# Residual additions moved to the end of DVE's step, and the last one split between ACT and POOL

## The chip, the cores and the metric

The kernel runs on one core of a Trainium2 chip. What is told is the device time of one execution in microseconds; lower is better. The core's engines work side by side: PE (TensorE) multiplies matrices, DVE (VectorE) and ACT (ScalarE) read and write SBUF and PSUM, POOL (GpSimd) works on SBUF, and SP (SyncE) issues transfers. Each runs its own list of instructions in order and waits on semaphores for the others.

## What is computed

x is 8 sequences of 512 tokens with 128 channels, all in float32. Two residual blocks follow each other. The first is a state space mixer with 32 heads, the second a feed-forward block that mixes each token with the one before it:

```python
x = L0_attn_x
x = x + _layernorm(_L0_attn_ref(_layernorm(x, axis=-1), ...), axis=-1)
x = x + _layernorm(_L0_ffn_ref(_layernorm(x, axis=-1), ...), axis=-1)

# in _L0_ffn_ref:
x_prev = jnp.concatenate([jnp.zeros((B, 1, C), x.dtype), x[:, :-1, :]], axis=1)
xr = mu_r * x + (1.0 - mu_r) * x_prev
xk = mu_k * x + (1.0 - mu_k) * x_prev
r = jax.nn.sigmoid(jnp.einsum('btc,dc->btd', xr, W_r))
k = jnp.einsum('btc,dc->btd', xk, W_k)
k_act = jnp.square(jax.nn.relu(k))
out = r * jnp.einsum('btc,dc->btd', k_act, W_v)
```

The mixer projects the normalised x to z (256 columns), a gated x (512), B and C (192) and per-head scalars, rotates B and C by accumulated angles, forms scores in chunks of tokens with a state carried from chunk to chunk, gates with z and projects back with W_out. The two layer norms of a block's result (`_layernorm(...)` behind each block) are what the names below call the factor of the first residual and the last normalisation.

## The kernel before, in words

**Tiles.** The tokens are cut in chunks of 64; a tile holds 64 tokens of two sequences on 128 partitions and 128 channels. There are 8 chunks c of 4 tiles (NQ = 4), 32 tiles n = 4 c + q. Each engine unrolls one `step` for each n. x, o (the projected result) and so on lie in SBUF for all tiles: `x_all`, `o_all`.

**The mixer, a pipeline over tiles.** In step n, PE projects x of tile n+1 (`project_x`, L876), turns B and C of tile n+1 (`turn`, L940, which waits for the mask of tile n), projects z, B and C of tile n+2 (`project_bc`, L868), turns y of n-1 (L1062), does the chunk's products of tile n (`mix`, L963 to L975), the scores of n+1 (L954), and the output product of n-1 (L1071), then a part of the feed-forward block. ACT in step n: copy and square of o (tile n-2, L693, L695), the gate of x of tile n+1 (`x_gate`, silu in PSUM, L667), `turned` (L678), the upper part of x of tile n+3 (L582), then a part of the feed-forward block (`empty_ffn_bank`), y turned (L683), squares of B and C of n+2 (L656, L658, behind DVE's `biased`), the gate of z (L673), the square of y (L688), and last `ffn(n)`. POOL in step n: the lower part of x (L430), `ffn(n)`, then factors of tile n+2 behind ACT's squares (L455, L458, L466), the scaling of z (`decayed_z`, L473), and the decay of the state (L481).

**DVE's step n, in order:** `mask` of tile n (L1405), `gated_y` of n-1 (L1424), `state` (L1413), `ffn(n)`, `weighted_x` x1 of tile n+1 (L1398, waits for ACT's gate and for POOL's factors), `biased` of n+2 (L1381), `weighted_x` xg of n+1 (L1398), in q = 3 `mix` (two instructions, L1509), and `rotations` of n+2 (two, L1386 and L1391, both with two inputs in SBUF).

**The feed-forward block, behind by chunks.** In step n = (c, q), DVE's `ffn` does: q = 0 `moments(c-2)` (L1488, L1490); q = 1 `norm_biases(c-2)` (L1499) and, from c = 4, `last_residual(c-4)` (L1531, four tiles: o_all = ff * rstd + x_all); q = 2 `factor_terms(c-1)`, `gated_v(c-3)` (L1518) and `stats3(c-3)` (L1525); q = 3 `residual(c-1)` (L1471, four tiles: x_all = o_all * factor + x_all) and `stats2(c-1)` (L1477), for c-1 from 0 to 5. `moments(k)` takes both the statistics of the residual of chunk k and those of the feed-forward result of chunk k-2; POOL raises them to -1/2 (`rstd`, L500), DVE forms the bias -mean * rstd. ACT's `ffn`: q = 0 `k_square`, q = 1 `normed(c-2)` (L731, scale and bias, four tiles), q = 2 `outputs(c-4)` (L774, four tiles: adds the bias to o_all), and in `empty_ffn_bank` q = 0 `k_relu`, q = 1 `gate_r`, q = 3 `scaled_behind(c-2)` (L746, two instructions). DVE's `mix(c-2)` in q = 3 waits for `scaled_behind`. PE in q = 3, after the step of the mixer, does `project_k` (L1114), which waits for `mix`; in q = 0 `project_r` (L1135).

**The end.** Chunk 7 is split in two units of two tiles, so there are 9 units; `residual(6)` stands behind step 30, and `last_ffn` on each engine holds what is left. `last_use(k)` and `rounds` say which earlier round used the columns of statistics that round k takes again, and so what `rstd`, `norm_biases` and `gated_v` wait for. SP stores a chunk when the count `outv` says that its four tiles are done.

## Time and profile before

| what | value |
|---|---|
| median of 3 runs | 247.10 us (246.79 to 247.14) |
| the profiled execution | 247.12 us |
| its span | 245.3 us |
| granted clock of PE, mean | 0.96 |
| busy: PE, DVE, ACT, POOL | 208.8, 210.7, 181.3, 142.4 us |

The page's second part shows the span in 40 slices, each digit the busy share in tenths:

```profile
PE   0895997589999999979979997999799799949930
PEld 0893443357777776758857875787588577627920
DVE  1799999987879987996999999999999998864880
ACT  2466685639988689778977896899789879747661
POOL 7444225646777696766757765766777576046230
```

The first 50 us load the inputs and build tables. From there to 211 us the 32 tiles run through the pipeline, with the granted clock at full. From about 120 us (chunk 3) every chunk has the same pattern. The last 34 us are the remainder of the feed-forward block. The chain that ended last, as the profile gives it, is only the last output operation, so the order of the waits has to be read from the timelines.

### The profile page before, as it was taken

The numbers are of one execution on the slowest core, as the hardware profiler recorded it, in microseconds if no ns is written. First come the engines' busy times: TensorE is split into PE (matmuls) and PEld (weight loads), VectorE is DVE, ScalarE is ACT, GpSimd is POOL, SyncE is SP. The second block draws the span as 40 slices with busy tenths as digits, with TensorE's granted clock in tenths as the row PEclk, the third lists the DMA queues.
The fourth block names the chain that finished last, engine by engine and source line by source line (L and its number), as shares of the span: only waits on it lengthen the run. The fifth ranks groups of instructions, "written<-read, shape, count | busy, mean of one in ns | idle before, by whom it ended". The sixth has DMA issues, their size and how long they took to land. (4 is left out here: it accounts for less than half of the span.)

```text
span 245.3 us, 6409 instructions
## 1 busy us (share of the span) xinstructions
PE 208.8 (85%) x1902; PEld 156.1 (64%) x1902; DVE 210.7 (86%) x658; ACT 181.3 (74%) x697; POOL 142.4 (58%) x241
## 2 busy tenths in 40 slices
PE   0895997589999999979979997999799799949930
PEld 0893443357777776758857875787588577627920
DVE  1799999987879987996999999999999998864880
ACT  2466685639988689778977896899789879747661
POOL 7444225646777696766757765766777576046230
PEclk9999799989999999999999999999999999986995
DMA  5980000000000000000000001001000100100223
GB/s 119 233 283 1 3 0 0 1 0 4 3 1 4 0 3 0 4 1 3 3 3 0 3 4 44 3 0 45 3 3 0 43 5 4 43 0 0 45 52 88
DMA packets 10199, 6.45 MB, mean 26 GB/s; under 512 B 864, under 2 KB 9856, under 8 KB 10160
## 3 DMA queue, kind: packets, MB, share of 16 engines
q1 hardware_dynamic: 10016, 5.77, 9.1%
q8 instruction: 18, 0.29, 0.5%
q0 software_dynamic: 144, 0.21, 0.4%
q14 instruction: 21, 0.17, 0.2%
HBM read 3.88 MB, written 2.10 MB: 24 GB/s over the span
## 5 line engine op out<-in xcount | busy, mean ns | idle before, releaser
L975 PE MATMUL bank<-x,sg 64*64 64x256 f32 x256 | 35.4, 396 | 0.0
L667 ACT ACTIVATE bank<-bank,rsn 128x512 f32<-128x512 f32 x32 | 21.1, 659 | 17.0 <-PE bank L876 17.0
L975 PE MATMUL bank<-xg,sg 64*64 64x256 f32 x256 | 33.0, 376 | 0.0
L963 PE MATMUL pair<-x,turned_bc 64*64 64x256 f32 x224 | 31.1, 397 | 0.0
L1398 DVE TENSOR_TENSOR x<-bank,wx 128x512 f32<-128x512 f32 x32 | 21.8, 682 | 7.3 <-ACT bank L667 7.3
L458 POOL TENSOR_TENSOR rb<-mse,halfn 128x2 f32<-128x2 f32 x32 | 24.8, 773 | 2.5
L500 POOL TENSOR_TENSOR frs<-fmo,halfn 128x8 f32<-128x8 f32 (+2 forms) x13 | 15.1, 1158 | 17.2 <-DVE fmo L1490 17.2
L1071 PE MATMUL bank<-wo_sb,yt 128*128 128x128 f32 x128 | 23.3, 306 | 1.9 <-ACT yt L683 1.9
L430 POOL TENSOR_TENSOR x_lo<-xnT_all,x_hi 128x128 fp32r<-128x128 f32 x32 | 14.8, 463 | 17.0 <-ACT x_hi L582 16.9
L656 ACT ACTIVATE junk<-bank 128x64 f32<-128x64 f32 x64 | 13.9, 228 | 11.2 <-DVE bc L1381 8.7
L975 PEld LDWEIGHTS bank<-xg,sg 64*64 64x64 f32 x256 | 18.0, 134 | 6.3 <-issue 0.2
L473 POOL TENSOR_TENSOR zs<-zs,ec_all 128x256 f32<-128x256 f32 x32 | 22.0, 687 | 0.0
L975 PEld LDWEIGHTS bank<-x,sg 64*64 64x64 f32 x256 | 15.4, 135 | 10.1 <-issue 6.1
L1398 DVE TENSOR_TENSOR xg<-bank,wx 128x512 f32<-128x512 f32 x32 | 21.7, 679 | 0.0
L455 POOL TENSOR_TENSOR mse<-msb,eps_all 128x2 f32<-128x2 f32 x32 | 7.4, 233 | 24.0 <-ACT junk L658 23.8
L481 POOL TENSOR_TENSOR st<-sp,f_all 128x256 f32<-128x256 f32 x28 | 18.1, 646 | 5.4 <-DVE sp L1413 5.4
L876 PE MATMUL bank<-w_hi,x_hi 128*128 128x512 f32 x32 | 17.2, 536 | 3.8 <-DVE w_lo L1282 2.7
L1071 PEld LDWEIGHTS bank<-wo_sb,yt 128*128 128x128 f32 x128 | 17.1, 194 | 4.7 <-ACT yt L683 2.1
L969 PE MATMUL bank<-st,bt 64*64 64x256 f32 x128 | 19.4, 379 | 0.6 <-DVE o_all L1333 0.6
L954 PEld LDWEIGHTS pair<-bt 64*64 64x64 f32 x256 | 16.9, 132 | 4.4
L954 PE MATMUL pair<-bt 64*64 64x64 f32 x256 | 18.0, 217 | 0.0
L1386 DVE TENSOR_TENSOR rot<-bc,cs_all 128x384 f32<-128x384 f32 x32 | 17.6, 550 | 0.0
(200 smaller groups left out, 712.0 us busy)
## 6 DMA issues: line engine op xcount, KB each, us to landing
x_all<-x SPq DMA_DIRECT2D x16, 128.0 KB, 3.7
out<-o_all SPq DMA_DIRECT2D x14, 128.0 KB, 2.5
cm<-consts SPq DMA_DIRECT2D x1, 640.0 KB, 5.6
w_sb<-w_in SPq DMA_DIRECT2D x1, 480.0 KB, 4.6
out<-o_all SPq DMA_DIRECT2D x4, 64.0 KB, 2.1
cm<-consts POOLq DMA_DIRECT2D x1, 128.0 KB, 3.9
wo_sb<-w_out SPq DMA_DIRECT2D x1, 128.0 KB, 4.7
bcb_sb<-bc_bias SPq DMA_DIRECT2D x1, 96.0 KB, 3.7
```

Of the source, the lines that this page charges most:

```text
L458: nc.gpsimd.tensor_tensor(rb[:, par], mse[:], halfn[:, 0:R], ALU.pow).then_inc(S["rb_ready"], 1)
L473: nc.gpsimd.tensor_tensor(zs[:, q].rearrange("p (h e) -> p h e", e=P), zs[:, q].rearrange("p (h e) -> p h e", e=P), at(ec_all, n).unsqueez ...
L481: nc.gpsimd.tensor_tensor(st[:, q].rearrange("p (h e) -> p h e", e=P), sp[:].rearrange("p (h e) -> p h e", e=P), at(f_all, i).unsqueeze(2) ...
L667: nc.scalar.activation(x_ps[:], x_ps[:], ACT.Silu, scale=rsn[:, par:par + 1]).then_inc(S["x_silu"], 1)
L876: mm = nc.tensor.matmul(x_ps[:], a[:, par], b[:, O_X:O_S], start=(k == 0), stop=(k == 2))
L954: mm = nc.tensor.matmul(scores[half(h), r], bt[half(r), par, r, half(h)], bt[half(r), par, 1 - r, half(h)], start=True, stop=True)
L963: mm = nc.tensor.matmul(p_ps[half(1 - h)], turned_bc[half(h), q, 2 * r], rx(x, r)[half(h)], start=(r == 0), stop=(r == R - 1))
L969: mm = nc.tensor.matmul(y_ps[par][half(h)], bt[half(1 - h), par, h, half(h)], state[half(1 - h)], start=True, stop=stop)
L975: mm = nc.tensor.matmul(y_ps[par][half(h)], sg[half(h), a, r], rx(x, r)[half(h)], start=start, stop=stop)
L1071: mm = nc.tensor.matmul(o_ps, yt[:, k], wo_sb[:, k], start=(k == 0), stop=(k == 1))
L1386: vec.tensor_tensor(rot[:], bc[:].rearrange("p (g a n) -> p g a n", g=G3, a=2).unsqueeze(3) .broadcast_to([128, G3, 2, 2, H]), at(cs_all, ...
L1398: vec.tensor_tensor((x1, xg)[a][:, par].rearrange("p (a e) -> p a e", e=P), x_ps[:].rearrange("p (a e) -> p a e", e=P), wx[:, par, a].unsq ...
```

## The change

- DVE's `residual(c-1)` leaves `ffn` in q = 3 and stands at the very end of DVE's step, behind `mix` and `rotations`.
- Its statistics, `stats2`, stand at the start of `ffn` in q = 0 of the next chunk, ahead of `moments`.
- For chunks 0, 1 and 2 (`POOL_UNITS = 3`) DVE's `last_residual` is not done. ACT, in place of `outputs`, writes the whole last normalisation `ff * rstd + bias` to o_all (`scaled_f`, four tiles), and POOL adds x_all to it (`add_residual`), two tiles in its `ffn` of q = 3 of the same chunk of steps and two in q = 1 of the next.
- The waits for `res`, the count of DVE's last residuals, are split by `wait_added`: for those chunks they are for ACT's new count `scaled_f`.
- All other work, and `last_ffn`, is as before.

```diff
--- before.py
+++ after.py
@@ -49,6 +49,7 @@
 
 FAC_STEPS = 3
 LAST_SPLIT = 2
+POOL_UNITS = 3
 MIX_UNITS = 6
 UNITS = [(c * NQ, c * NQ + NQ) for c in range(NC_ - 1)] + [(NT - NQ, NT - NQ + LAST_SPLIT), (NT - NQ + LAST_SPLIT, NT)]
 
@@ -293,7 +294,7 @@
         wv_half = sb("wv_half", 128, D)
         ff = sb("ff", 128, 2 * NQ, D)
         cnames = ("x1 stats agg mom pow norm_bias normed tr_ps tr_sb carried shifted scaled mixed last k_ps k_relu k_act r_ps th "
-                  "v_ps f stats3 res outv").split()
+                  "v_ps f stats3 scaled_f res outv").split()
         C = {n: sem("c_" + n) for n in cnames}
         s_mix = sem("mixing_weights")
         s_wo = sem("w_out_centred")
@@ -369,8 +370,15 @@
 
             for j in range(k - 1, -1, -1):
                 if rounds[j][0] < rounds[k][1] and rounds[k][0] < rounds[j][1]:
-                    return j + 1, hi(rounds[j][2]), hi(rounds[j][3])
-            return 0, 0, 0
+                    return j + 1, hi(rounds[j][2]), rounds[j][3]
+            return 0, 0, -1
+
+        def wait_added(eng, u):
+
+            if u < POOL_UNITS:
+                wait_past(eng, C["scaled_f"], hi(u))
+            else:
+                eng.wait_ge(C["res"], hi(u) - hi(POOL_UNITS - 1))
 
         def aggregated(k):
 
@@ -495,7 +503,7 @@
                 pool.wait_ge(C["mom"], k + 1)
                 wait_past(pool, C["norm_bias"], used)
                 wait_past(pool, C["normed"], n2)
-                wait_past(pool, C["res"], n3)
+                wait_added(pool, n3)
                 t = slice(rounds[k][0], rounds[k][1])
                 nc.gpsimd.tensor_tensor(frs[:, t], fmo[:, t], halfn[:, 0:t.stop - t.start], ALU.pow).then_inc(C["pow"], 1)
 
@@ -512,11 +520,17 @@
                 nc.gpsimd.tensor_tensor(prevT[:, B:, 0:1], curT[:, 0:B, L - 1:L],
                                         one[:].unsqueeze(1).broadcast_to([128, B, 1]), ALU.mult).then_inc(C["carried"], 1)
 
+            def add_residual(u, part):
+                for i in range(lo(u), hi(u))[part]:
+                    pool.wait_ge(C["scaled_f"], i + 1)
+                    pool.wait_ge(C["x1"], i + 1)
+                    nc.gpsimd.tensor_tensor(o_all[:, i], o_all[:, i], x_all[:, i], ALU.add).then_inc(C["outv"], 1)
+
             def pool_outputs(u, part):
                 pool.wait_ge(C["norm_bias"], round3(u) + 1)
                 pool.wait_ge(C["outv"], lo(u) + part.start)
                 for i in range(lo(u), hi(u))[part]:
-                    pool.wait_ge(C["res"], i + 1)
+                    pool.wait_ge(C["res"], i + 1 - hi(POOL_UNITS - 1))
                     nc.gpsimd.tensor_scalar(o_all[:, i], o_all[:, i], fnb[:, column3(i):column3(i) + 1], None,
                                             ALU.add).then_inc(C["outv"], 1)
 
@@ -528,6 +542,10 @@
                     carry_scaled(c - 2)
                 if q == 2 and valid(c - 1):
                     factors(c - 1)
+                if q == 3 and 0 <= c - 4 < POOL_UNITS:
+                    add_residual(c - 4, slice(0, 2))
+                if q == 1 and 0 <= c - 5 < POOL_UNITS:
+                    add_residual(c - 5, slice(2, 4))
 
             def last_ffn():
                 rstd(6)
@@ -766,11 +784,19 @@
                 act.wait_ge(C["k_relu"], u + 1)
                 nc.scalar.activation(ka[:, columns(u)], ka[:, columns(u)], ACT.Square).then_inc(C["k_act"], 1)
 
+            def scaled_f(u):
+                act.wait_ge(C["norm_bias"], round3(u) + 1)
+                act.wait_ge(C["x1"], hi(u))
+                for i in range(lo(u), hi(u)):
+                    k = column3(i)
+                    nc.scalar.activation(o_all[:, i], ff[:, slot(i)], ACT.Identity, scale=frs[:, k:k + 1],
+                                         bias=fnb[:, k:k + 1]).then_inc(C["scaled_f"], 1)
+
             def outputs(u):
                 act.wait_ge(C["norm_bias"], round3(u) + 1)
                 act.wait_ge(C["outv"], lo(u))
                 for i in range(lo(u), hi(u)):
-                    act.wait_ge(C["res"], i + 1)
+                    act.wait_ge(C["res"], i + 1 - hi(POOL_UNITS - 1))
                     nc.scalar.activation(o_all[:, i], o_all[:, i], ACT.Identity,
                                          bias=fnb[:, column3(i):column3(i) + 1]).then_inc(C["outv"], 1)
 
@@ -810,7 +836,7 @@
                 if q == 1 and valid(c - 2):
                     normed(c - 2)
                 if q == 2 and valid(c - 4):
-                    outputs(c - 4)
+                    (scaled_f if c - 4 < POOL_UNITS else outputs)(c - 4)
 
             act.wait_ge(S["st_zero"], 2)
             for n in range(-2, NT):
@@ -1494,7 +1520,9 @@
                 used, n2, n3 = last_use(k)
                 dve.wait_ge(C["pow"], k + 1)
                 wait_past(dve, C["normed"], n2)
-                wait_past(dve, C["outv"], n3)
+                wait_added(dve, n3)
+                if n3 >= POOL_UNITS:
+                    dve.wait_ge(C["outv"], hi(n3))
                 t = slice(rounds[k][0], rounds[k][1])
                 vec.scalar_tensor_tensor(out=fnb[:, t], in0=fag[:, t, 0], scalar=-1.0, in1=frs[:, t], op0=ALU.mult,
                                          op1=ALU.mult).then_inc(C["norm_bias"], 1)
@@ -1513,7 +1541,7 @@
             def gated_v(u):
                 dve.wait_ge(C["th"], u + 1)
                 dve.wait_ge(C["v_ps"], u + 1)
-                wait_past(dve, C["res"], hi(ahead(u)))
+                wait_added(dve, ahead(u))
                 for k, i in enumerate(range(lo(u), hi(u))):
                     vec.scalar_tensor_tensor(out=ff[:, slot(i)], in0=th[:, slot(i)], scalar=1.0,
                                              in1=ffn_bank("v", u)[:, k * D:k * D + D],
@@ -1534,19 +1562,18 @@
             def ffn(n):
                 c, q = divmod(n, NQ)
                 if q == 0 and valid(c - 2):
+                    if c - 2 < NC_ - 2:
+                        stats2(c - 2)
                     moments(c - 2)
                 if q == 1 and valid(c - 2):
                     norm_biases(c - 2)
-                if q == 1 and valid(c - 4):
+                if q == 1 and valid(c - 4) and c - 4 >= POOL_UNITS:
                     last_residual(c - 4)
                 if q == 2 and valid(c - 1):
                     factor_terms(c - 1)
                 if q == 2 and valid(c - 3):
                     gated_v(c - 3)
                     stats3(c - 3)
-                if q == 3 and 0 <= c - 1 < NC_ - 2:
-                    residual(c - 1)
-                    stats2(c - 1)
 
             def last_ffn(general):
                 stats2(6)
@@ -1609,6 +1636,8 @@
                     mix(n // NQ - 2)
                 if within(n + 2):
                     rotations(n + 2, (q + 2) % NQ)
+                if q == NQ - 1 and 0 <= n // NQ - 1 < NC_ - 2:
+                    residual(n // NQ - 1)
 
             biased(0)
```

## Rows read from the trace of the kernel before

**Rows 1.** The windows view: stretch, length, busy time of PE, PEld, DVE, ACT, POOL.

```profile
140.00:160.00 20.00, 18.72 (x199) 14.13 (x199) 19.86 (x60) 16.76 (x72) 13.98 (x24) 1.00 0.07 16
```

**Rows 2.** The waits view, 77 to 200 us: total idle, times, longest.

```profile
DVE x L1398 <- ACT bank L667: 4.1, 4, 1.8
...
PE bank L1114 <- DVE prevT L1509: 6.6, 5, 1.4
```

**Rows 3.** The timeline of DVE, chunk 3, q=1: start, duration, instruction, [idle before].

```profile
114.06 0.69 DVE L1398 TENSOR_TENSOR x<-bank,wx 128x512 f32<-128x512 f32 x1 [1.79 <-ACT bank L667]
```

**Rows 4.** The timeline of DVE, chunk 4 and the start of chunk 5.

```profile
134.45 2.03 DVE L1531 SCALAR_TENSOR_TENSOR o_all<-ff,frs,x_all 128x128 f32<-128x128 f32 x4
...
136.40 0.68 DVE L1398 TENSOR_TENSOR x<-bank,wx 128x512 f32<-128x512 f32 x1
...
138.72 0.42 DVE L1405 TENSOR_TENSOR sg<-pair,cm 128x256 f32<-128x256 f32 x1
...
141.96 0.67 DVE L1398 TENSOR_TENSOR x<-bank,wx 128x512 f32<-128x512 f32 x1
...
142.55 0.35 DVE L1381 TENSOR_TENSOR bc<-bank,bcb_sb 128x192 f32<-128x192 f32 x1
...
145.26 1.89 DVE L1471 SCALAR_TENSOR_TENSOR x_all<-o_all,tokc,x_all 128x128 f32<-128x128 f32 x4
...
147.07 0.86 DVE L1477 BATCH_NORM_STATS2 fst<-x_all 128x6 f32<-128x128 f32 x4
...
147.85 0.67 DVE L1398 TENSOR_TENSOR x<-bank,wx 128x512 f32<-128x512 f32 x1
...
149.30 0.74 DVE L1509 SCALAR_TENSOR_TENSOR curT<-bank,mu_sb,behind 128x512 f32<-128x512 f32 x1
...
151.56 0.41 DVE L1405 TENSOR_TENSOR sg<-pair,cm 128x256 f32<-128x256 f32 x1
...
152.56 0.63 DVE L1488 BATCH_NORM_AGGREGATE fag<-fst 128x2 f32<-128x6 f32 x8
...
153.38 0.69 DVE L1398 TENSOR_TENSOR x<-bank,wx 128x512 f32<-128x512 f32 x1
...
156.78 2.04 DVE L1531 SCALAR_TENSOR_TENSOR o_all<-ff,frs,x_all 128x128 f32<-128x128 f32 x4
```

**Rows 5.** The timeline of ACT, the same stretch.

```profile
135.60 0.66 ACT L667 ACTIVATE bank<-bank,rsn 128x512 f32<-128x512 f32 x1 [0.78 <-PE bank L876]
...
139.04 1.64 ACT L731 ACTIVATE dt_all<-x_all,fnb,frs 128x128 f32<-128x128 f32 x4
...
142.93 0.22 ACT L656 ACTIVATE junk<-bank 128x64 f32<-128x64 f32 x1 [0.52 <-DVE bc L1381]
...
144.55 1.27 ACT L774 ACTIVATE o_all<-o_all,fnb 128x128 f32<-128x128 f32 x4
...
146.12 0.66 ACT L667 ACTIVATE bank<-bank,rsn 128x512 f32<-128x512 f32 x1
...
147.16 1.28 ACT L746 ACTIVATE behind<-bank,one_less_mu 128x512 f32<-128x512 f32 x2
...
154.48 0.24 ACT L656 ACTIVATE junk<-bank 128x64 f32<-128x64 f32 x1
...
156.95 0.21 ACT L695 ACTIVATION_READ_ACCUMULATOR junk_o<-bank 128x1 f32 x1
```

**Rows 6.** The timeline of PE, end of chunk 4 and start of chunk 5.

```profile
150.75 1.12 PE L1114 MATMUL bank<-curT,wk_sb 128*128 128x512 f32 x2 [1.28 <-DVE prevT L1509]
...
152.43 0.38 PE L940 MATMUL pair<-cm,turned_bc 128*128 128x128 f32 x2
```

**Rows 7.** The view by tile, x_all, the residual's line: durations min/median/max in ns.

```profile
L1471 DVE SCALAR_TENSOR_TENSOR x_all<-o_all,tokc,x_all x32: 338/347/728, 81.3 to 222.8; 128x128 f32<-128x128 f32 x32
```

**Rows 8.** The timeline of DVE, last chunk, the residual while POOL stands idle.

```profile
210.04 1.13 DVE L1471 SCALAR_TENSOR_TENSOR x_all<-o_all,tokc,x_all 128x128 f32<-128x128 f32 x4
```

**Rows 9.** The timeline of POOL: scaling of z at the start of chunk 5.

```profile
151.39 0.74 POOL L473 TENSOR_TENSOR zs<-zs,ec_all 128x256 f32<-128x256 f32 x1
```

## Prediction

> **What bounds the kernel now.** I read the windows first. In the steady stretch DVE is busy 19.86 us of 20 and PE 18.72 [rows 1], so the busiest engine is DVE. Then the waits: between 77 and 200 us the only large wait of PE is 6.6 us in 5 pieces, and it ends with DVE's mixed tokens (L1509) [rows 2]. The reader should see that both engines are nearly full, and that each chunk has one place where PE stands still for DVE.
>
> Third, the DVE timeline of one chunk. It repeats every 22.33 us (the last residual starts at 134.45 and 156.78 [rows 4]). I number the steps of a chunk q=0 to 3; q=3 starts just before 145.26, q=0 with the mask at 151.56. Two questions follow. What would DVE meet if the four last residual additions of q=1 were not there? Chunk 3 answers: it has none, and in the same place DVE stands idle 1.79 us for ACT's gate of x [rows 3]. With the additions the time from then to the next step is nearly the same: they fill a hole. So their removal is worth little by itself. What does the residual of q=3 cost? It stands ahead of the mixing, so the mixing ends late and PE waits 1.28 us in front of project_k [rows 6].
>
> **The change part by part.** I follow each chain by start-to-start distances, in the clock of the chunk shown.
>
> (a) Four last residuals off DVE in chunks 4, 5, 6: 12 instructions, 2.03 us for four [rows 4], 6 us of DVE time; on the path nearly nothing by the hole above, unless DVE is late, which is part (c).
>
> (b) Residual (1.81 us, 145.26 to 147.07) and its statistics (0.78, 147.07 to 147.85) leave the place before x1 [rows 4]. DVE is then free at 145.26, 2.59 us earlier. But x1 needs ACT's gate of x, which runs 146.12 to 146.78, behind the four output operations that start at 144.55 [rows 5]. These become scale-and-bias activations like the second normalisation (L731): 1.64 for four instead of 1.27, +0.37. So the gate ends at 147.15. After it ACT computes the shifted tokens (L746): 147.16 + 0.37 = 147.53, + 1.28 = 148.81, and the mixing can't start before 148.84. It started at 149.30. Of the 2.59 us only 0.46 arrives; PE's wait shrinks by that, not to nothing.
>
> (c) What is late next. From the start of the mixing to the next mask 2.26 us pass (149.30 to 151.56 [rows 4]). Now the residual of four tiles stands in between. Its price R: four take 1.13 us undisturbed [rows 8], 1.05 start to start; in the steady stretch 1.81, because single ones take up to 728 ns instead of 347 [rows 7] while POOL works. At the new place POOL's scaling of z (0.74 us, 151.39 [rows 9]) overlaps: one blocked instruction rather than two, so R = 1.5; ends 1.05 and 1.81. The mask then starts at 148.84 + 2.26 + 1.5 = 152.6, 1.04 later than before. PE's turning of B and C needs that mask; it started at 152.43, the mask ended at 151.97 [rows 4, 6]: 0.46 us of slack. PE is therefore later by some 0.6 us there, more than it gained.
>
> (d) Does it recover? The ring from mask to mask of the next chunk, which now passes DVE and ACT by turns: mask to moments 1.00, statistics 0.78 (moved here), moments 0.82, x1 and the bias product 0.94, together 3.54; ACT from squares to the end of its step 2.68 (154.48 to 157.16 [rows 5]); gate 0.66; DVE x1 to mask 2.32, mask to x1 of q=3 3.24 and its bias product 0.94 [rows 4]; ACT squares to outputs 1.62, outputs to gate 1.57 + 0.37, gate to shifted tokens 1.04, these 1.28 [rows 5]; mixing to mask 2.26; residual 1.50; and four hand-overs of 0.03 (142.90 to 142.93 [rows 4, 5]). Sum 23.14 us, against 22.33 now: +0.81 a chunk. Before, the same ring without statistics, residual and 0.37 was 20.5 and did not bind; DVE's 1.95 us of removed work can't be used, since DVE stands waiting for ACT twice in the ring.
>
> The ring holds in full from the mask of chunk 4 to that of chunk 7: three times 0.81 = 2.43 us. In chunks 1 to 3 ACT has no outputs, the ring is 23.14 - 1.53 = 21.6, PE binds, and the earlier mixing and the later mask cancel: 0, between -0.8 (three times the 0.45 by which R may be smaller, less what PE can't use) and +0.4.
>
> (e) The 12 additions on POOL stand in q=3 (two) and q=1 (two). No row shows this form; the nearest is POOL's scaling of z, 0.74 us for 256 columns [rows 9], and a tile has 128, so between 0.37 and 0.74 each; I take 0.45, 1.8 us a chunk. POOL is idle for 6.02 of 20 us [rows 1], 6.7 a chunk, so its own work is hidden; without that cover it would be the whole 1.8. The output transfers that it delays land long before the end. But two of them at q=1 fall on DVE's rotation, whose inputs both lie in SBUF like the residual's: an estimate of 0.2 us a time (ends 0, no overlap, and 0.5, two blocked), three times, 0.6.
>
> The Trainium skill, SBUF — State Buffer, Who interferes with whom, says that a DVE instruction with two SBUF inputs contends with a GpSimd instruction that reads SBUF and fully blocks. The residual's 347 and 728 ns agree [rows 7]; by the rule each pair of additions on POOL could block rotation and its sum in turn, which is the upper end, 0.5.
>
> (f) The last chunk has no moved residual, its last residual stays on DVE; a delay passes to the tail, which is a chain. PE was at first 0.46 behind the mask, so up to 0.4 of the delay is slack.
>
> **Sum.** 2.43 + 0.6 + 0 - 0.35 = 2.7 us. The profiled execution took 247.12 us (span 245.3 and 1.8 around it), as good as the median 247.10. Forecast 249.8.
>
> **Rivals.** A, the busiest engine decides: DVE is the fullest [rows 1], so what leaves it leaves the time, 3 x 1.96 = 5.9 us: 241.2. For it: 19.86 of 20 us. Against: the 1.79 us hole where the work was not [rows 3]. The Trainium skill, Perfetto Trace Analysis, Identifying the Most-Contended Engine, tells to optimise the engine of highest occupancy first; by that this change would pay.
>
> B, PE decides and its wait goes: the five waits of 6.6 us [rows 2] vanish and the later mask meets slack: 240.5. It decides in favour if the mask of q=0 starts before 151.97, that is if the mixing starts before 148.2 at R = 1.5; it needs ACT 0.6 us earlier than I have it. A half of it, 244, is as likely as the whole.
>
> C, the two effects cancel: R = 1.05 and no collision with POOL. The ring is 22.69, three times 0.36 = 1.1, less 0.8 from chunks 1 to 3: 247.4.
>
> D, contention in full: R = 1.81 and 0.5 each time. Ring 23.45 + 0.5: 3 x 1.62 + 0.4 - 0.35 = 4.9: 252.0.
>
> **How the numbers follow.** Forecast (249.8, its own range 248.0 to 251.3) 0.60; D 0.08; C 0.14; A 0.05; B whole or half 0.13. What a measurement can tell from no change is about 0.2%, 0.5 us: C gives 0.1 to "same" and 0.04 to slower. Slower 0.60 + 0.08 + 0.04 = 0.72, same 0.10, faster 0.18. The range: 246.0 to 251.8 leaves out A, nearly all of B and D's end, about 0.2.
>
> **What the profile of after would show.** (b) right: the x1 of q=3 in chunks 4 to 6 waits 1.5 us or more for ACT L667 or its successor; PE's wait before project_k is shorter than 1.28 but not gone. (c): the residual between turned B/C and mask takes 1.3 to 1.8 us, and PE has a new wait in q=0 for the mask. (d): masks of q=0 are 23.1 us apart or more, and x1 of q=1 waits for ACT. (e): a rotation of 550 ns lengthened where POOL adds. What would make it wrong: ACT's outputs and gate earlier than reckoned (an ACT wait in q=3 that I took for work), or DVE catching up at q=1; then masks are 21 us apart and PE's waits disappear.

## The result and the profile after

The changed kernel takes 251.58 us (median of 4 runs, 250.85 to 252.37), beside 247.06 us for the kernel before: ratio 1.0185, interval 1.0146 to 1.0225. The change makes the kernel slower by 4.5 us; forecast were 2.7 us, to 249.8. The measured time lies 0.3 us above the forecast's own range (248.0 to 251.3) and 0.2 us inside the whole range, which reaches to 251.8. The profiled execution of after took 251.0 us (span 248.7), that of before 247.12 (span 245.3): 3.9 us, and 3.4 in the span. The two were not granted the same mean clock, 0.964 in after and 0.960 in before, and step (f) below comes back to that.

The first view of after is busy time, where [rows 1] showed DVE at 19.86 us of 20: first the totals over the span, then the windows view (stretch, length, busy time of PE, PEld, DVE, ACT, POOL).

```profile
PE 208.8 (84%) x1902; PEld 154.9 (62%) x1902; DVE 205.8 (83%) x646; ACT 182.4 (73%) x697; POOL 146.5 (59%) x253
...
140.00:160.00 20.00, 18.10 (x181) 13.33 (x179) 16.94 (x56) 16.20 (x67) 13.80 (x25) 1.00 0.01 2
```

DVE is busy 2.9 us less in these 20 us and is no longer the fullest engine, yet PE does less in them as well, 18.10 instead of 18.72 us. A part of that is the place of the window in the chunk. From the mask of chunk 5 to that of chunk 6 the same view gives for before 22.34 us with PE busy 21.07 and DVE 22.14 (151.48 to 173.82), for after 23.67 us with 21.34 and 20.57 (152.96 to 176.63). Over this chunk DVE is rid of 1.6 us, PE has 0.3 us more, and no engine is full. So the time has gone into waits. The waits view of after, 77 to 204 us (total idle, times, longest), gives them.

```profile
DVE x L1424 <- ACT bank L685: 13.1, 13, 1.8
...
PE pair L966 <- DVE sg L1431: 5.7, 6, 1.0
PE bank L1088 <- ACT junk_o L713: 2.3, 4, 0.8
...
PE bank L1140 <- DVE prevT L1537: 1.8, 5, 0.5
```

L1424 is the x of L1398 before, L1140 is L1114, L1537 is L1509. PE's wait for the mixed tokens fell from 6.6 us to 1.8 [rows 2], and in its place stand 5.7 us in front of the turned B and C for DVE's mask and 2.3 us for ACT. DVE's own waits for ACT's gate of x rose from 4.1 us (5.0 up to 204 us) to 13.1. That is the ring of step (d): DVE stands for ACT, then PE and ACT stand for DVE.

The DVE timeline of one chunk shows it (start, duration, instruction, [idle before]).

```profile
147.53 0.69 DVE L1424 TENSOR_TENSOR x<-bank,wx 128x512 f32<-128x512 f32 x1 [1.83 <-ACT bank L685]
...
149.19 0.75 DVE L1537 SCALAR_TENSOR_TENSOR curT<-bank,mu_sb,behind 128x512 f32<-128x512 f32 x1
...
151.38 1.65 DVE L1497 SCALAR_TENSOR_TENSOR x_all<-o_all,tokc,x_all 128x128 f32<-128x128 f32 x4
152.96 0.41 DVE L1431 TENSOR_TENSOR sg<-pair,cm 128x256 f32<-128x256 f32 x1
...
153.95 0.86 DVE L1503 BATCH_NORM_STATS2 fst<-x_all 128x6 f32<-128x128 f32 x4
155.01 0.64 DVE L1514 BATCH_NORM_AGGREGATE fag<-fst 128x2 f32<-128x6 f32 x8 [0.20 <-DVE fst L1503]
...
155.77 0.69 DVE L1424 TENSOR_TENSOR x<-bank,wx 128x512 f32<-128x512 f32 x1
...
160.01 0.69 DVE L1424 TENSOR_TENSOR x<-bank,wx 128x512 f32<-128x512 f32 x1 [0.76 <-ACT bank L685]
...
162.06 0.50 DVE L1417 TENSOR_TENSOR turned_bc<-rot 128x192 f32<-128x192 f32 x1
162.48 0.41 DVE L1431 TENSOR_TENSOR sg<-pair,cm 128x256 f32<-128x256 f32 x1
...
163.55 0.36 DVE L1488 TENSOR_TENSOR tokc<-csq_all,eps_all 128x4 f32<-128x4 f32 x1
163.95 0.55 DVE L1490 SCALAR_TENSOR_TENSOR tokc<-tokc 128x4 f32<-128x4 f32 x1
...
166.00 0.67 DVE L1424 TENSOR_TENSOR x<-bank,wx 128x512 f32<-128x512 f32 x1
...
176.63 0.41 DVE L1431 TENSOR_TENSOR sg<-pair,cm 128x256 f32<-128x256 f32 x1
```

DVE stands idle 1.83 us in front of x1 of q=3, where the residual had been [rows 4]; then the residual stands between turned B and C and the mask; then DVE waits again in q=1, where the last residuals had been. PE, at the same place as in [rows 6]:

```profile
150.66 1.12 PE L1140 MATMUL bank<-curT,wk_sb 128*128 128x512 f32 x2 [0.46 <-DVE prevT L1537]
...
153.51 0.41 PE L966 MATMUL pair<-cm,turned_bc 128*128 128x128 f32 x2 [1.03 <-DVE sg L1431]
```

Where 1.28 us stood before project_k there are 0.46, and 1.03 us are new in front of the turning. The two waits together, 1.49, are more than the one of before.

The distance from mask to mask of q=0 is the ruler for all that follows. Its columns below: chunks 4 to 5, 5 to 6, 6 to 7, and their sum, read off the starts of the mask's line in each profiled execution; then the median time and the ratio to before with its interval.

| kernel | 4-5 | 5-6 | 6-7 | sum | us | ratio |
|---|---|---|---|---|---|---|
| before | 22.33 | 22.34 | 22.33 | 67.00 | 247.06 | |
| after | 23.26 | 23.67 | 23.78 | 70.71 | 251.58 | 1.0185 (1.0146 to 1.0225) |
| e1_move_only | 24.10 | 24.10 | 24.12 | 72.32 | 253.19 | 1.0255 (1.0227 to 1.0283) |
| e2_split_only | 22.23 | 22.66 | 22.67 | 67.56 | 247.75 | 1.0047 (1.0027 to 1.0066) |
| e3_residual_behind_mask | 23.09 | 23.52 | 23.61 | 70.22 | 251.54 | 1.0185 (1.0155 to 1.0214) |
| e4_no_pool_adds | 23.24 | 23.23 | 23.33 | 69.80 | 250.87 | 1.0170 (1.0138 to 1.0201) |
| e5_act_norm_in_q3 | 22.35 | 22.51 | 22.52 | 67.38 | 248.64 | 1.0068 (1.0036 to 1.0100) |
| e6_both | 22.22 | 22.22 | 22.32 | 66.76 | 247.77 | 1.0046 (1.0024 to 1.0068) |
| e7b_old_place_stats_late | 21.48 | 22.25 | 22.38 | 66.11 | 244.87 | 0.9926 (0.9900 to 0.9953) |
| e8_reordered | 21.79 | 22.24 | 22.74 | 66.77 | 245.53 | 0.9964 (0.9939 to 0.9989) |
| e9_reordered_all_dve | 23.65 | 23.62 | 23.64 | 70.91 | 248.70 | 1.0102 (1.0061 to 1.0142) |
| e10b_adds_before_state | 21.80 | 22.04 | 22.12 | 65.96 | 244.90 | 0.9932 (0.9909 to 0.9955) |
| e11b_residual_old_place | 21.81 | 22.04 | 22.14 | 65.99 | 244.85 | 0.9913 (0.9884 to 0.9941) |
| e12_old_place_adds_moved | 21.47 | 21.96 | 22.04 | 65.47 | 244.31 | 0.9900 (0.9876 to 0.9924) |

Each experiment ran beside the kernel before on its chip; those medians lie between 246.55 and 246.88, so a ratio compares better than a time. What lies around the three distances, for the kernels that need it, in us: the start of the mask of q=0 in chunks 1, 4 and 7, the stretch from chunk 1 to 4, and the rest of the span behind the mask of chunk 7.

| kernel | chunk 1 | chunk 4 | chunk 7 | 1 to 4 | rest |
|---|---|---|---|---|---|
| before | 67.67 | 129.23 | 196.23 | 61.56 | 49.1 |
| after | 67.91 | 129.70 | 200.41 | 61.79 | 48.3 |
| e1_move_only | 68.33 | 130.12 | 202.44 | 61.79 | 49.0 |
| e3_residual_behind_mask | 67.96 | 128.26 | 198.48 | 60.30 | 51.2 |
| e5_act_norm_in_q3 | 68.65 | 130.44 | 197.82 | 61.79 | 49.2 |
| e6_both | 67.90 | 128.23 | 194.99 | 60.33 | 50.9 |
| e7b_old_place_stats_late | 68.11 | 127.77 | 193.88 | 59.66 | 49.4 |

Ahead of the mask of chunk 1 the engines' orders are those of before in every kernel, and the starts still lie up to 1.5 us apart (67.19 in e9, 67.67 in before, 68.65 in e5). After's span difference of 3.4 us is then 0.24 from there, 0.23 from chunks 1 to 4, 3.7 from the three distances, and 0.8 less in the rest. In e3 and e6 the residual stands behind the mask, so their rest holds one residual more than the others'.

### The profile page after: what moved, and what is told of

Its sections match the earlier page's. It is cut to its first block and busy times, and to the rows that moved or that the text cites. A ratio compares the mean times of both kernels' runs of the same rounds, so it can differ in the third digit from the quotient of the medians.

```text
span 248.7 us, 6422 instructions
## 1 busy us (share of the span) xinstructions
PE 208.8 (84%) x1902; PEld 154.9 (62%) x1902; DVE 205.8 (83%) x646; ACT 182.4 (73%) x697; POOL 146.5 (59%) x253
## 5 line engine op out<-in xcount | busy, mean ns | idle before, releaser
L1424 DVE TENSOR_TENSOR x<-bank,wx 128x512 f32<-128x512 f32 x32 | 22.0, 688 | 15.6 <-ACT bank L685 15.6
L1001 PE MATMUL bank<-x,sg 64*64 64x256 f32 x256 | 34.6, 389 | 0.0
L989 PE MATMUL pair<-x,turned_bc 64*64 64x256 f32 x224 | 30.3, 389 | 0.0
L1424 DVE TENSOR_TENSOR xg<-bank,wx 128x512 f32<-128x512 f32 x32 | 21.8, 680 | 0.0
L481 POOL TENSOR_TENSOR zs<-zs,ec_all 128x256 f32<-128x256 f32 x32 | 20.7, 648 | 0.0
L966 PE MATMUL pair<-cm,turned_bc 128*128 128x128 f32 x64 | 12.5, 277 | 9.4 <-DVE sg L1431 9.3
L966 PEld LDWEIGHTS pair<-cm,turned_bc 128*128 128x128 f32 x64 | 8.0, 140 | 17.1 <-issue 13.8
L463 POOL TENSOR_TENSOR mse<-msb,eps_all 128x2 f32<-128x2 f32 x32 | 8.1, 253 | 17.2 <-ACT junk L676 17.2
```

The source lines that it names most:

```text
L481: nc.gpsimd.tensor_tensor(zs[:, q].rearrange("p (h e) -> p h e", e=P), zs[:, q].rearrange("p (h e) -> p h e", e=P), at(ec_all, n).unsqueez ...
L966: mm = nc.tensor.transpose(t_ps[:, 128 * k:128 * k + 128], turned_bc[:, q, k:k + 2].rearrange("p g n -> p (g n)"), c_("ident"))
L989: mm = nc.tensor.matmul(p_ps[half(1 - h)], turned_bc[half(h), q, 2 * r], rx(x, r)[half(h)], start=(r == 0), stop=(r == R - 1))
L1001: mm = nc.tensor.matmul(y_ps[par][half(h)], sg[half(h), a, r], rx(x, r)[half(h)], start=start, stop=stop)
L1424: vec.tensor_tensor((x1, xg)[a][:, par].rearrange("p (a e) -> p a e", e=P), x_ps[:].rearrange("p (a e) -> p a e", e=P), wx[:, par, a].unsq ...
```

## The experiments

**One half at a time.** The change has two parts: the last residuals of three chunks leave DVE for ACT and POOL, and the residual of q=3 with its statistics moves behind mixing, rotation and mask. e1_move_only keeps the second alone, e2_split_only the first.

```diff
# e1_move_only
-POOL_UNITS = 3
+POOL_UNITS = 0
# e2_split_only: residual and statistics back at their old place
                 if q == 0 and valid(c - 2):
-                    if c - 2 < NC_ - 2:
-                        stats2(c - 2)
...
+                if q == 3 and 0 <= c - 1 < NC_ - 2:
+                    residual(c - 1)
+                    stats2(c - 1)
...
-                if q == NQ - 1 and 0 <= n // NQ - 1 < NC_ - 2:
-                    residual(n // NQ - 1)
```

> The moved residual with its statistics alone; all last residuals stay on DVE and the output operations on ACT as before. Theory (the ring through DVE and ACT decides): at q=1 the path of DVE from one x1 to the next is now 2.32 + 1.0 + 0.08 + 1.96 = 5.4 us where ACT's was 4.3, so the ring is 1.0 longer than in the whole change, and 0.4 shorter by ACT's cheaper outputs and without POOL's collisions: about 24.0 us from mask to mask, 5 us over before: 252. Rival (the split between ACT and POOL is what costs, the move is free or pays): 241 to 247.

> The split of the last residual alone; the residual stays in its old place ahead of the mixing. Theory: the removed DVE time opens the 1.8 us hole of chunk 3 again, so nothing is gained there; POOL's additions cost DVE 0.4 us in two or three chunks: 247.5 to 248.2. Rival (the fullest engine decides, so DVE's 6 us are the gain and the move alone is the loss): 241 to 243.

e1: 24.10 us from mask to mask and 253.19 us. The ring is as expected, the time 1.2 us over. Its DVE timeline in q=1 has the four last residuals with no idle before x:

```profile
160.44 2.15 DVE L1559 SCALAR_TENSOR_TENSOR o_all<-ff,frs,x_all 128x128 f32<-128x128 f32 x4
162.51 0.68 DVE L1424 TENSOR_TENSOR x<-bank,wx 128x512 f32<-128x512 f32 x1
```

The move alone costs 6.5 us beside before's 246.73; in the profiled execution 5.3 of 6.1 us lie in the three distances and 0.66 ahead of the mask of chunk 1. In this ring DVE is late at q=1, so the additions there are paid for: without them (after) the three distances and the time are both 1.6 us less.

e2: 247.75 us, as expected. In before's order the additions stood in a hole, and the hole is there when they are gone:

```profile
159.07 0.69 DVE L1424 TENSOR_TENSOR x<-bank,wx 128x512 f32<-128x512 f32 x1 [1.78 <-ACT bank L685]
```

1.78 us, as the 1.79 of [rows 3]. DVE is rid of 6 us of work and the kernel is slower by 0.47%. Rival A, that the fullest engine decides (241.2), is refuted, and with it, for this kernel, the advice that the prediction quotes beside it: the same half of the change is worth -1.0 us in one order and 1.6 in the other.

**Is it the late mask?** The residual can stand behind the mask instead of ahead of it.

```diff
# e3_residual_behind_mask
                     if c - 2 < NC_ - 2:
+                        residual(c - 2)
                         stats2(c - 2)
...
-                if q == NQ - 1 and 0 <= n // NQ - 1 < NC_ - 2:
-                    residual(n // NQ - 1)
```

> The whole change, but the moved residual stands in q=0 behind mask, y and state and ahead of its statistics, so that the mask is not delayed. Theory (ring): the residual is still between the mixing and x1 of q=0, the ring keeps its length but for a little contention: 250.4 to 251.6. Rival (the late mask, for which PE waits 1.03 us a chunk, is what costs): 3 us less or more, 247 to 248.5.

The time is the same, 251.54, as expected. The mask is earlier, and PE's wait for it nearly disappears (waits view, 77 to 204 us, then DVE's timeline):

```profile
PE pair L966 <- DVE sg L1431: 1.3, 5, 0.3
```

```profile
151.35 0.42 DVE L1431 TENSOR_TENSOR sg<-pair,cm 128x256 f32<-128x256 f32 x1
...
152.35 1.51 DVE L1497 SCALAR_TENSOR_TENSOR x_all<-o_all,tokc,x_all 128x128 f32<-128x128 f32 x4
...
155.60 0.69 DVE L1424 TENSOR_TENSOR x<-bank,wx 128x512 f32<-128x512 f32 x1
```

The x of step q=0 starts 4.25 us behind the mask, where it was 2.81 in after (155.77 - 152.96). The 1.5 us have moved from one side of the mask to the other, and the sum of the three distances is 70.22 instead of 70.71; the earlier mask of chunk 4 is given back in the rest. PE's wait for the mask, 5.7 us in total, was a sign and not the cost: the residual lies on the ring through DVE wherever it stands between the mixing and that x.

**Do POOL's additions cost?** e4 leaves the addition of x out of the output of chunks 0 to 2; ACT's activation releases the transfer.

```diff
# e4_no_pool_adds (wait_added waits for outv in place of scaled_f)
-                    add_residual(c - 4, slice(0, 2))
+                    pass
...
-                    add_residual(c - 5, slice(2, 4))
+                    pass
...
-                                         bias=fnb[:, k:k + 1]).then_inc(C["scaled_f"], 1)
+                                         bias=fnb[:, k:k + 1]).then_inc(C["outv"], 1)
```

> The whole change without the 12 additions on POOL: x is left out of the output of chunks 0 to 2. Theory: the additions push DVE's sum of the rotation by 0.14 and its factor terms by 0.28 us in three chunks, so 1.2 us less than with them: about 250.2. Rival (POOL's additions are hidden): no difference. Rival (they are most of the loss): 248.

250.87 us, 0.7 less, where I expected 1.2; the intervals of e4 and after overlap, so the time alone doesn't settle it. The distances do: 23.23 and 23.33 instead of 23.67 and 23.78. The same three instructions, in e4's clock:

```profile
162.46 0.36 DVE L1417 TENSOR_TENSOR turned_bc<-rot 128x192 f32<-128x192 f32 x1
...
163.80 0.15 DVE L1488 TENSOR_TENSOR tokc<-csq_all,eps_all 128x4 f32<-128x4 f32 x1
163.99 0.48 DVE L1490 SCALAR_TENSOR_TENSOR tokc<-tokc 128x4 f32<-128x4 f32 x1
```

They took 0.50, 0.36 and 0.55 in after. POOL's timeline of after shows what ran beside them:

```profile
161.15 1.19 POOL L527 TENSOR_TENSOR o_all<-o_all,x_all 128x128 f32<-128x128 f32 x2
...
163.48 0.41 POOL L474 TENSOR_TENSOR wx<-w_all,rb 128x128 f32<-128x128 f32 x1
```

The first meets the turned B and C, one of the two instructions that the prediction had in its way. The other, the rotation, kept its 0.55 us (161.48 in after); beside it the two additions took 1.19 us instead of the 0.88 that they take elsewhere, so there it was POOL that stood. The second is no addition at all: it is POOL's old scaling of w, which the additions have pushed to where DVE's factor terms are. The collision costs 0.44 us a time in the distances, where I had taken 0.2.

**Can ACT leave the ring?** In after ACT computes the last normalisation in q=2 (144.91 to 146.45), ahead of the gate that x1 of q=3 waits for (146.86). In e5 it does so in q=3. e6 is e3 and e5 together.

```diff
# e5_act_norm_in_q3 (ACT; POOL's additions go to q=0 and q=1)
-                if q == 2 and valid(c - 4):
-                    (scaled_f if c - 4 < POOL_UNITS else outputs)(c - 4)
+                if q == 3 and 0 <= c - 4 < POOL_UNITS:
+                    scaled_f(c - 4)
+                if q == 2 and valid(c - 4) and c - 4 >= POOL_UNITS:
+                    outputs(c - 4)
```

> The whole change, but ACT's four scale-and-bias operations of a chunk stand at the end of ACT's step q=3 instead of q=2 (and POOL's additions in q=0 and q=1). Theory (ring): they leave the ring, which passes ACT's step q=2 but has 2.5 us of slack behind step q=3. The ring falls from 23.3 to 23.8 by up to 1.53, to 22.0 to 22.3, three times: 246.5 to 247.7. Rival (ACT's place doesn't matter, DVE's late residual alone costs): 250 to 251.6.

> As the kernel with ACT's operations in q=3, and the moved residual behind mask, y and state in q=0. Theory: the ring no longer holds PE so far back, so the mask that is 1.5 us earlier now counts a little: 245.8 to 247.3. Rival (mask never matters): as the kernel with ACT's operations in q=3.

e5: 248.64 us, 2.9 less than after; right in direction, 1 us short of what I expected, with distances of 22.35 to 22.52. DVE's wait before x1 of q=3 in the next chunk:

```profile
169.89 0.69 DVE L1426 TENSOR_TENSOR x<-bank,wx 128x512 f32<-128x512 f32 x1 [0.53 <-ACT bank L685]
```

1.83 us have become 0.53, so 1.3 of the 1.54 us that the four activations held up the gate arrive. In its profiled execution 1 us lies ahead of the mask of chunk 1, which the change can't have caused: DVE's first instruction starts at 6.05 us there, at 5.05 in before. e6: 247.77, just outside what I expected; its distances (22.22, 22.22, 22.32) are below before's, and yet it is 0.5% slower: the mask of chunk 7 starts 1.24 us earlier than before's, and the rest, with the residual in it, is 1.8 longer.

**The residual at its old place, without the statistics.** e7b is e5 with the residual back ahead of x1 of q=3, and the statistics left in q=0. With ACT's gate earlier, what did the old place cost?

```diff
# e7b_old_place_stats_late, against e5
+                if q == 3 and 0 <= c - 1 < NC_ - 2:
+                    residual(c - 1)
...
-                if q == NQ - 1 and 0 <= n // NQ - 1 < NC_ - 2:
-                    residual(n // NQ - 1)
```

> The split with ACT's operations in q=3, the residual back in its old place ahead of x1, and only its statistics in q=0. Theory (ring): statistics, moments and the bias product stay in one row behind the mask of q=0, so the ring is about 22.0 to 22.2 us, 0.2 to 0.3 under before, with 0.4 for POOL's collisions in it: 246 to 247.3. Rival (the residual's place alone decides, and the old one is as good as before): 246.6, the time before; the two can hardly be told apart, so the distance of the masks is what counts here: 22.1 against 22.3.

244.87 us, better than I had expected, and faster than before. Against e5 only the residual's place differs: 248.64 and 244.87, 3.8 us (3.5 by the ratios, for they ran beside different runs of before); in the profiled executions 2.13 of them lie in chunks 1 to 4 (61.79 and 59.66) and 1.27 in the three distances. From chunk 1 to 4 there is no last normalisation in either kernel, so e7b differs there from before in the statistics' place alone, and is 1.9 us faster (61.56 and 59.66). That half of the move was a gain; in after the residual eats it (61.79). Behind the mask of chunk 4 the distance is 21.48, with no addition of POOL in it, then 22.25 and 22.38 with two pairs in each.

**Everything behind the rotation.** e8 does two tiles of the residual ahead of x1 and two at the end of the step, moves statistics, moments and biases of q=0 and q=1 behind the rotations too (the factor terms of q=2 stay), and lets POOL add four tiles in q=0 and take its powers in q=1. e9 is e8 with POOL_UNITS = 0.

```diff
# e8_reordered, DVE (called at the end of a step)
+            def end_of_step(n):
+                c, q = divmod(n, NQ)
+                if q == 3 and 0 <= c - 1 < NC_ - 2:
+                    residual(c - 1, slice(2, 4))
                 if q == 0 and valid(c - 2):
...
# POOL
+                if q == 0 and 0 <= c - 5 < POOL_UNITS:
+                    add_residual(c - 5, slice(0, 4))
+                if q == 1 and valid(c - 2):
                     rstd(c - 2)
```

> The work of the change in another order: two tiles of the residual in q=3 ahead of x1, where DVE waits for ACT's gate, two at the step's end; statistics and moments at the end of q=0, behind the rotation; biases and last residual at the end of q=1; POOL's powers in q=1 and its additions in q=0; ACT's operations in q=3. Theory: nothing of the feed-forward block is then between the mask of q=0 and the bias product that ACT waits for, the ring is under PE's 21 us, and the chunks take 21.0 to 21.6 us instead of 22.3: 242 to 244.5. Rival (some other wait of the same size appears, the period of 22.3 is robust): 246 to 248.

> The same order with all last residuals on DVE and the output operations on ACT in q=2. Theory: the order takes the ring away, so DVE's own work of 22.1 us a chunk is the bound in chunks 4 to 6 and the 2 us of a last residual count in full now: 2 to 4 us slower than with the split, 245.5 to 247.5. Rival (the split is worth nothing in any order): the same as with it.

e8: 245.53 us with distances of 21.79 to 22.75; expected were 21.0 to 21.6, a miss. Two things stand in its trace. PE waits for the mask nine times (waits view), and the rotation beside POOL's additions takes 0.83 us instead of 0.55:

```profile
PE pair L966 <- DVE sg L1431: 4.8, 9, 0.9
```

```profile
174.91 0.83 DVE L1412 TENSOR_TENSOR rot<-bc,cs_all 128x384 f32<-128x384 f32 x1
175.78 0.49 DVE L1417 TENSOR_TENSOR turned_bc<-rot 128x192 f32<-128x192 f32 x1
```

e9: 248.70, 3.2 us more than e8, also outside what I expected. It changes two things at once: with POOL_UNITS = 0 DVE has the last residuals again, and ACT has its output additions in q=2 again, ahead of the gate. Which of the two costs the 3.2 us it doesn't tell.

**Another place for the additions.** e10b, e11b and e12 set them at the end of POOL's step, ahead of the state; e10b from e8, e11b from e10b with the residual whole at its old place, e12 from e7b.

```diff
# e12_old_place_adds_moved, against e7b (POOL)
-                if q == 0 and 0 <= c - 5 < POOL_UNITS:
-                    add_residual(c - 5, slice(0, 2))
...
-                if q == 1 and 0 <= c - 5 < POOL_UNITS:
-                    add_residual(c - 5, slice(2, 4))
...
                     decayed_z(n + 2, (q + 2) % NQ)
+                if q == 3 and 0 <= n // NQ - 4 < POOL_UNITS:
+                    add_residual(n // NQ - 4, slice(0, 2))
+                if q == 0 and 0 <= n // NQ - 5 < POOL_UNITS:
+                    add_residual(n // NQ - 5, slice(2, 4))
```

> The reordered kernel with POOL's additions at the end of its steps q=3 and q=0, ahead of the state's decay, where POOL stands waiting for DVE's sum and DVE runs operations with one input in PSUM. Theory: the masks of chunks 5 to 7, 22.2 and 22.7 us apart with the additions beside the rotation (which took 0.84 instead of 0.55 us), come back to 21.8 as in chunks 3 to 5: 1.2 us less, 244.0 to 244.8. Rival (the additions are hidden, another work fills these chunks): 245.5.

> As the kernel with POOL's additions moved, with all four tiles of the residual in their old place ahead of x1. Theory: two tiles fit in DVE's wait for ACT's gate, the other two push the mixing back 0.6 to 0.9 us, and PE's wait before project_k grows by that while its wait for the mask, 0.5, goes: 0 to 0.4 us a chunk more, 244 to 246. Rival (DVE's total work alone counts now): no difference.

> The split with ACT's operations in q=3, the residual in its old place, its statistics in q=0, and POOL's additions at the end of POOL's steps q=3 and q=0. Theory: the masks of chunks 5 to 7, which were 22.25 and 22.38 us apart with the additions ahead of DVE's rotation and factor terms, come back towards the 21.5 of chunk 4 to 5, where no addition in q=1 runs: 0.5 to 1.4 us less than 244.9, 243.5 to 244.4. Rival (the additions are not what fills these chunks): 244.9.

e10b: 244.90 us, 0.1 over what I expected. e11b: 244.85, no difference, as the distances (65.96 and 65.99) say too; that is what its rival said, and the growth of PE's wait that I expected didn't come. e12: 244.31 us, as expected, ratio 0.9900, the lowest median here: 1.0% below before and 7 us below after. Its interval overlaps those of e7b, e10b and e11b; against e7b the distances say the same as the time (65.47 and 66.11). Its DVE and POOL in the middle of chunk 5:

```profile
158.02 0.36 DVE L1419 TENSOR_TENSOR turned_bc<-rot 128x192 f32<-128x192 f32 x1
...
159.36 0.36 DVE L1490 TENSOR_TENSOR tokc<-csq_all,eps_all 128x4 f32<-128x4 f32 x1
159.76 0.56 DVE L1492 SCALAR_TENSOR_TENSOR tokc<-tokc 128x4 f32<-128x4 f32 x1
```

```profile
159.29 0.42 POOL L474 TENSOR_TENSOR wx<-w_all,rb 128x128 f32<-128x128 f32 x1
```

The turned B and C are free again (0.36); the factor terms still meet POOL's scaling of w, 0.29 us more for the two than in e4, start to start. A second thing is longer in the same chunk, the residual of q=3. The first row is chunk 4, with the distance of 21.47, the second chunk 5, with 21.96:

```profile
143.36 1.89 DVE L1499 SCALAR_TENSOR_TENSOR x_all<-o_all,tokc,x_all 128x128 f32<-128x128 f32 x4
...
165.12 2.09 DVE L1499 SCALAR_TENSOR_TENSOR x_all<-o_all,tokc,x_all 128x128 f32<-128x128 f32 x4
```

0.29 and 0.20 are the 0.49 us between these two distances; the sum fits, but no run took either away. The windows view, as above, has PE, ACT and POOL fuller than in either kernel and DVE between the two; from the mask of chunk 5 to that of chunk 6, PE is busy 20.85 and DVE 20.77 of 21.96 us. DVE's waits for the gate are down to 4.7 us, from 13.1 in after:

```profile
140.00:160.00 20.00, 19.38 (x215) 15.26 (x215) 18.80 (x56) 18.02 (x77) 16.58 (x30) 1.00 0.06 13
```

```profile
DVE x L1426 <- ACT bank L685: 4.7, 7, 1.2
...
PE bank L1142 <- DVE prevT L1539: 4.2, 5, 1.2
```

## Why the prediction was right in direction and small in size

**Step (a), the removal is worth nearly nothing: right**, for before's order (e2; there it costs 0.47% rather than nothing, and the distances behind the mask of chunk 5 are 0.32 and 0.34 longer, with the same collisions as in after: 0.49, 0.36 and 0.56 for the three instructions). Where DVE is late, as in (c) and (d), it is worth something, and 1.6 us is its size there (e1 against after). The step named that condition and gave it no price.

**Step (b), only a part of the 2.59 us arrives: right.** The mixing starts 19.49 us behind the mask of its chunk (149.19 - 129.70), before 20.07 (149.30 - 129.23): 0.58 earlier, forecast 0.46. x1 waits 1.83 us for ACT, forecast 1.5 or more. ACT's scale-and-bias activations take 1.64 us for four, as taken from the second normalisation. PE's wait is shorter and not gone.

**Step (c), the price of the residual at its new place: right.** From mixing to mask 3.77 us pass (152.96 - 149.19), forecast 2.26 + 1.5 = 3.76. The new wait of PE for the mask is there, 1.03 us.

**Step (d), the ring: right, with two terms mis-sized.** That chunks 1 to 3 cancel is right too: 61.79 us instead of 61.56. The second distance of after, link by link; the steps named are those in which the instruction stands (what the prediction's sum calls the x1 of q=3, at 3.24, is the x of step q=2):

| link | forecast | measured |
|---|---|---|
| mask to DVE's x, step q=0 | 2.60 | 2.81 |
| to ACT's squares | 0.97 | 0.99 |
| squares to gate | 2.68 | 2.55 |
| gate to DVE's x, step q=1 | 0.69 | 0.70 |
| x to mask of q=2 | 2.32 | 2.47 |
| mask to x, step q=2 | 3.24 | 3.52 |
| to ACT's squares, to outputs, to gate | 4.53 | 4.54 |
| gate to shifted tokens, these, to mixing | 2.35 | 2.34 |
| mixing to mask, with the residual | 3.76 | 3.75 |
| sum | 23.14 | 23.67 |

Two links carry the error. The first, 0.21: I had moved the statistics from one place of the sum to another with their old duration. At the old place x1 and the rest of the step stood between the statistics and the aggregation that reads them; at the new one they stand next to each other, and DVE waits 0.20 us for its own last statistics (the row at 155.01). The row of before for the statistics [rows 4] couldn't show that; the order of the new code gave reason to ask. The order alone doesn't make the wait, though. In the rounds of chunks 2 and 3 the same two stand next to each other without it:

```profile
87.11 0.86 DVE L1503 BATCH_NORM_STATS2 fst<-x_all 128x6 f32<-128x128 f32 x4
88.00 0.38 DVE L1514 BATCH_NORM_AGGREGATE fag<-fst 128x2 f32<-128x6 f32 x4
```

Those rounds aggregate four columns and wait for the count `stats` alone; from chunk 4 on a round has eight, of both kinds, and waits for `stats` and `stats3`. Which of these makes the 0.20 us wasn't tried. The second error, 0.15 + 0.28 in the links x to mask and mask to x, is the collision with POOL of step (e).

**Step (e), the collision: mechanism right, place half right, size half.** I looked for DVE instructions beside the additions, and found the rotation, which was not lengthened, and its sum, which was, by 0.15 us. I didn't ask what the additions push further back on POOL. The scaling of w, pushed onto the factor terms, makes 0.28 of the 0.43 us. The rule of the Trainium skill, SBUF — State Buffer, Who interferes with whom, that DVE with two SBUF inputs and a reading POOL block each other, agrees with all three instructions, also with that of 4 columns (0.15 to 0.36 us).

**Step (f), the slack: not shown.** I took off 0.35. The part behind the mask of chunk 7 is 0.8 us shorter than before's (48.3 and 49.1), but that isn't shown to be slack: e2, with the residual at its old place, has 48.2 there. These four part by the granted clock, whose mean behind the mask of chunk 7 is 0.89 in after and e2 and 0.87 in before and e1; between before and e1, which are alike in it, 0.1 us is left (49.07 and 48.96), though e1 is 6 us late. The clock isn't all of it either, for e4, at 0.89 and with after's order there, has 48.8.

Together, for the profiled executions: forecast 2.7, measured 3.9 (3.4 in the span). The three rings hold 3.71 us of it where I had 2.43 and two times 0.2; that is 0.9 short: 0.36 by the first link less the small ones (23.26 in the distance without a collision, against 23.14, three times), 0.46 in the collision (two times 0.43 against two times 0.2), and less than 0.1 spread. The terms of the forecast that were mis-sized are thus the statistics' link in (d) and the collision in (e).

The median of after is 0.6 us above its profiled execution, and the clock goes with that as well. Of the four runs of after two had a mean granted clock of 0.964 and took 250.85 and 251.00 us, two had 0.960 and took 252.16 and 252.37. The thirteen runs of before beside e1 to e4 part in the same way, at 0.964 or more (nine, mean 246.5 us) and at 0.960 or less (four, mean 247.4). Compared at the like clock the change costs 4.4 to 4.8 us. The three distances lie where both kernels were granted the clock in full, so they don't hang on it. They and what lies ahead of them make 4.2 us; where the rest of the 4.4 to 4.8 lies the runs don't show.

Rival B (PE's wait goes, 240.5 or 244) was refuted by the same rows: its condition was a mixing 0.6 us earlier than forecast, and it came 0.12 earlier (0.58 instead of 0.46). The rival's half, 244, is reached by e12, but not in the rival's way: there the residual is back at its old place, and PE's wait for the mixed tokens is 4.2 us and not gone. Rival C (the effects cancel, 247.4) fell with R, 1.58 and not 1.05. Rival D (252.0, by contention in full) lies nearer to the measured 251.58 than the forecast does, and that is luck: the price of the collision was nearly right, 0.44 of 0.5, but it gave the three distances 4.86 us more, with a residual of 1.81, where 3.71 were measured, with one of 1.58, and it didn't have the aggregation's wait.

**What is open.** Why the part ahead of the mask of chunk 1 differs by up to 1.5 us between kernels that have the same order there; it is a part of what e1 and e5 missed their expected times by. In e5 it is there from DVE's first instruction on. Why the granted clock falls for a longer time in some executions of a kernel than in others. Which of its two changes costs e9 its 3.2 us, and what e12's distances would be without the longer factor terms and residual, wasn't tried.

## What to carry to other kernels

An engine that is busy 99% of the time needn't be the one that sets it. Ask of each piece of work that is to be removed or moved what its engine would do in its place: if it would wait for another engine all that time, the gain is nothing (e2), and if it lies between a hand-over received and one given, all of it is a link of the ring, as the residual's 1.58 us in after. Here the same residual cost 3.8 us more behind the mixing, where the ring goes through it (e5), than at its old place (e7b), where DVE would have waited 0.53 us for ACT's gate anyway.

When work moves to a helper engine, follow that engine's whole queue, for it pushes its old work onto other instructions; and when an instruction comes to stand directly behind the one whose result it reads, don't take over the old duration unasked.

## What the runs showed of the hardware

A DVE instruction on 4 columns with two SBUF inputs takes 0.36 us instead of 0.15 while POOL's 128x128 product runs: 0.2 us more for next to no data. The rotation on 384 columns went from 0.55 to 0.83 us beside POOL's additions in e8 and kept its 0.55 beside them in after, and these take 0.88 us for two, or 1.19 where DVE meets them, where I had taken 0.9. A DVE aggregation directly behind the statistics that it reads waits 0.20 us for them in the rounds of chunks 4 to 7 of after (4 times in the stretch from 77 to 204 us), and doesn't in those of chunks 2 and 3, where it starts 0.03 us behind their end (87.11 + 0.86, then 88.00). Two executions of after at a mean granted clock of 0.960 took 1.3 us more than two at 0.964.
